# Attention scores of two heads at once on the row halves of the PE array, and no stacked copies of the queries

## The chip, the cores and the metric

The kernel runs on one core of one Trainium2 chip. The metric is the time of the whole program on the device, in microseconds (us). Lower is better. "PE" is TensorE, "DVE" VectorE, "ACT" ScalarE, "POOL" GpSimd, "SP" SyncE, which here only starts DMAs.

## The reference, cut to what matters

A pre-norm block: attention with grouped queries and rotary position, then a small quantized feed-forward layer. The change touches only the scores.

```python
B, S, E = (4, 512, 256);  H, KVH, D = (32, 8, 64)
q = (x @ Wq).reshape(b, s, H, D).transpose(0, 2, 1, 3)      # x is layer-normed
k = (x @ Wk).reshape(b, s, KVH, D).transpose(0, 2, 1, 3)
q = apply_rope(q, pos);  k = apply_rope(k, pos)
scores = einsum('bhqd,bhkd->bhqk', q, k) / sqrt(D)          # each k head serves 4 q heads
scores = where(causal, scores, finfo.min)
out = einsum('bhqk,bhkd->bhqd', softmax(scores), v) ...  @ Wo
```

A head has 64 dimensions, so the sum that makes one score runs over 64 values, while the PE array has 128 rows.

## The kernel before

**Work.** There are 32 steps, one for each batch and each group of four query heads that share one key head. A step has 16 units: four query tiles of 128 queries by four heads. The query tiles are taken in the order 0, 3, 2, 1 (`QUERY_TILES`, L21), and causality lets tile i see (i+1)*128 keys, so units 0 to 3 have n = 128 score columns, 4 to 7 have 512, 8 to 11 have 384 and 12 to 15 have 256. Two steps (`par` 0 and 1) make one pass of a loop, and buffers alternate with `par`.

**Precision.** The scores are wanted at nearly full float32 from products that keep fewer bits (type float32r). So queries and keys are each split in a high and a low part. `kT` holds the keys of the step on 128 partitions, as a high and a low tile. The 64 key dimensions are there twice, in partitions 0 to 63 and again in 64 to 127, because the host puts the key weights twice into the weight matrix. One projection tile j (0 or 1) of the queries holds two heads, 2j in partitions 0 to 63 and 2j+1 in 64 to 127.

**The stack.** Before, `keep_high` (ACT, L637) and `keep_low` (POOL, L351) write the two query parts to a staging area in `wv` (`query_parts`, L95). `place_queries` (SP, L247 to L260) then copies, with four DMAs for a tile, so that `qT[:, h, :]` has the high part of head h in partitions 0 to 63 and the low part in 64 to 127. One product over 128 rows with the high keys (L476) then gives (q_high + q_low) k_high, and a second (L477) gives (q_high + q_low) k_low. A third product (L478, bfloat16, 128 columns) adds the causal mask.

**A unit's way.** PE makes the scores into one of four banks `s_bank`. DVE takes the row maxima (L856). ACT makes the exponentials (L664), and reads the sums. PE transposes the probabilities (`turn`, L490). ACT keeps their high part (L673), DVE the low part (L849). PE multiplies them with the values (`attend`, L503). After every fourth unit DVE normalises the output of the query tile (L865, L870), PE transposes it (`turn_output`, L515), ACT and DVE split it (L681, L878), PE multiplies it with the output weights (`out_product`, at L410), and DVE adds the product to the residual (L888).

**Order.** Each engine's order is written out by hand. In unit u of a step PE issues `scores(u+3)` (LAG is 3; from u = 13 on these are units 0, 1, 2 of the next step), `turn(u)`, at u = 0, 4, 8, 12 the `out_product` of an earlier tile, `attend(u-2)`, at u = 1, 2, 5 the projection of tile 0, 1 or 2 of the next step (`project`, at L410), and at u = 2, 6, 10, 14 `turn_output`. DVE issues at u `keep_probT_low(u-1)` and `maxima(u+3)`. ACT issues `keep_probT(u)`, `exponentials(u+2)`, and after a projection `keep_raw` (L625), which moves it out of the single bank `x_bank`. `project`, `out_product` and `keep_raw` share that bank in turn. A projected tile is rotated: SP swaps its halves (L244), DVE multiplies by the cosines (L818), POOL by the sines (L342) and adds (L345).

**Waits of the scores.** `scores(u)` waits until the exponentials of unit u-4 have read the bank (`exp_done >= U-3`), at u = 0 for the low part of the keys, at u = 0 and 2 for the stacked queries (`q_placed`).

Of the kernel before, what the change touches and what calls it, by code (L numbers as in the profile page):

```python
# [7 lines left out]
GROUP_HEADS = HEADS // KV_HEADS  # L8
LN_EPS, QUANT_EPS, QUANT_MAX = 1e-5, 1e-7, 127.0
P = 128  # L10
# [6 lines left out]
KEYS = 2  # L17
# [33 lines left out]
def attention_ffn_kernel(nc: bass.Bass, x: bass.AP, w_group: bass.AP, w_value: bass.AP, w_out: bass.AP,  # L51
# [9 lines left out]
    with ctx:  # L61
# [6 lines left out]
        def sem(name):  # L68
            return ctx.enter_context(nc.semaphore(name))
# [24 lines left out]
        swp = [sb(f"swp{n}", [P, SEQ], f32)[:, :] for n in range(PROJ_TILES)]  # L94
        def query_parts(it, par, j):  # L95


            if isinstance(it, int) and (it, par) == (0, 0):
                return qT[1][:, j, :], qT[1][:, 2 + j, :]
            return wv[:, HI, j, :], wv[:, LO, j, :]  # L100

# [57 lines left out]
        rope_first, rope_second, rope_done, hi_kept, lo_kept = sem("rope_first"), sem("rope_second"), sem("rope_done"), sem("hi_kept"), sem("lo_kept")  # L159
        q_placed = [sem(f"q_placed{n}") for n in range(2)]  # L160
        scores_done, max_done, exp_done = sem("scores_done"), sem("max_done"), sem("exp_done")
# [27 lines left out]
        def tile_no(it, par, j):  # L189

            return it * (2 * PROJ_TILES) + (PROJ_TILES * par + j), j, it * 2 + par
# [14 lines left out]
        def query_tile(v):  # L206
            return QUERY_TILES[v]
# [11 lines left out]
        def _(sp):  # L219
# [26 lines left out]

            def place_queries(it, par, j):  # L247

                T, _, _ = tile_no(it, par, j)

                sp.wait_ge(lo_kept, T + 1)
                if isinstance(it, int) and (it, par) == (0, 1):
                    sp.wait_ge(q_placed[1 - j], 64)
                    sp.wait_ge(q_placed[j], 64)
                q_hi, q_lo = query_parts(it, par, j)
                for a in range(2):
                    h = 2 * j + a
                    rows = slice(64 * a, 64 * a + 64)
                    sp.dma_start(qT[par][0:64, h, :].bitcast(f32), q_hi[rows, :].bitcast(f32)).then_inc(q_placed[j], 16)
                    sp.dma_start(qT[par][64:128, h, :].bitcast(f32), q_lo[rows, :].bitcast(f32)).then_inc(q_placed[j], 16)  # L260

            def projected(it, par):
                for j in range(PROJ_TILES):
                    swap_halves(it, par, j)
                place_queries(it, par, 0)
                place_queries(it, par, 1)

# [15 lines left out]
        def _(pool):  # L283
# [63 lines left out]
            def keep_low(it, par, j):  # L347
                T, ring, _ = tile_no(it, par, j)
                pool.wait_ge(hi_kept, T + 1)
                high, low = (kT[par][:, HI, :], kT[par][:, LO, :]) if j == KEYS else query_parts(it, par, j)  # L350
                nc.gpsimd.tensor_tensor(low, raw[ring][:, :], high.bitcast(f32), ALU.subtract).then_inc(lo_kept, 1)  # L351
# [44 lines left out]
        def _(pe):  # L396
# [69 lines left out]
            def scores(it, par, u):  # L466
                i, h = query_tile(u // GROUP_HEADS), u % GROUP_HEADS
                U, n = unit_no(it, par, u), (i + 1) * P
                if not (isinstance(U, int) and U < 4):
                    pe.wait_ge(exp_done, U - 3)  # L470
                if u == 0:
                    pe.wait_ge(lo_kept, tile_no(it, par, KEYS)[0] + 1)
                if u in (0, 2):
                    pe.wait_ge(q_placed[h // 2], it * 128 + (64 * par + 64))
                bank, q = s_bank[(par * UNITS + u) % 4], qT[par][:, h, i * P:(i + 1) * P]
                nc.tensor.matmul(bank[:, 0:n], q, kT[par][:, HI, 0:n], start=True, stop=False)  # L476
                nc.tensor.matmul(bank[:, 0:n], q, kT[par][:, LO, 0:n], start=False, stop=False)  # L477
                nc.tensor.matmul(bank[:, i * P:n], ident_b[:, :], mask[:, :], start=False, stop=True)\  # L478
                    .then_inc(scores_done, 1)

# [44 lines left out]
            pe.wait_ge(xT_lo, TOK_TILES)  # L525
            for u in range(LAG):
                scores(0, 0, u)

            def step(it, par, first, last):
# [3 lines left out]
                for u in range(UNITS):  # L533
                    if u + LAG < UNITS:
                        scores(it, par, u + LAG)
                    elif not last:
                        scores(nit, npar, u + LAG - UNITS)
# [61 lines left out]
        def _(act):  # L599
# [28 lines left out]
            def keep_high(it, par, j):  # L628
                T, ring, _ = tile_no(it, par, j)
                act.wait_ge(rope_done, T + 1)  # L630
                if not (isinstance(it, int) and it == 0):
                    act.wait_ge(scores_done, unit_no(it, par, -UNITS))

                if j < KEYS and not (isinstance(T, int) and T < PROJ_TILES):
                    act.wait_ge(q_placed[j], it * 128 + 64 * par)
                dst = kT[par][:, HI, :] if j == KEYS else query_parts(it, par, j)[0]
                nc.scalar.activation(dst, raw[ring][:, :], ACT.Copy).then_inc(hi_kept, 1)  # L637
# [379 lines left out]
```

## Time and profile before

| what | value |
|---|---|
| time, median of 3 runs | 1007.95 us (1007.88 to 1008.24) |
| profiled execution, first to last instruction | 1007.3 us |
| PE busy | 864.6 us (86%), 8488 products and 8488 weight loads |
| DVE busy | 788.5 us (78%) |
| ACT busy | 670.0 us (67%) |
| POOL busy | 564.7 us (56%) |
| stacking copies (`qT<-wv` and `qT<-qT`) | 256 DMAs of 128 KB, 2.3 us each from issue to landing |
| scores on PE, L476, L477, L478 | 195.3, 164.7 and 117.8 us in the records |

The page gives no time for the profiled execution other than its span, which is 0.65 us below the median of the runs. Products on PE are pipelined, so that the duration in a record includes the way through the array and overlaps the next product. What a product costs is the distance between the start of its record and the start of the next one. "PEld" is the load of the weights (the stationary operand), which runs beside products. "Idle before" is the time that an engine stood still ahead of an instruction, with what ended it.

### The profile page before, as it was taken

What the parts mean: (1) busy time and instruction counts of PE and PEld (TensorE: products, weight loads), DVE (VectorE), ACT (ScalarE), POOL (GpSimd) and SP (SyncE); (2) the same over time, 40 slices, a digit from 0 to 9 for tenths busy, and PEclk for the clock granted to TensorE, in tenths of its full rate; (3) what the DMA queues carried; (4) which work ended last, traced back from release to release, by engine and by line L of the source; (5) the groups of instructions that cost most, each with busy time, mean ns of one, the idle gap of its engine ahead of it and who ended that gap; (6) DMA issues with size and microseconds to landing.
All of it is one profiled execution on the core that took longest, in us unless ns stands there. A gap on an engine that the chain in (4) does not pass through costs nothing.

```text
span 1007.3 us, 28110 instructions
## 1 busy us (share of the span) xinstructions
PE 864.6 (86%) x8488; PEld 699.2 (69%) x8488; DVE 788.5 (78%) x1869; ACT 670.0 (67%) x1954; POOL 564.7 (56%) x492
## 2 busy tenths in 40 slices
PE   2978999899999999999999999999999999998732
PEld 1757777677777777777777777777777777777511
DVE  5768878777877787887777777878777777778797
ACT  1557777676667677777766676777767766777533
POOL 4146666555566666655555656666555556554026
PEclk7899999999999999999999999999999999999855
DMA  7134334333333333343433343343434333432002
GB/s 232 42 83 92 91 80 95 74 88 78 86 91 90 82 86 91 78 93 74 91 76 88 89 91 83 81 94 78 94 73 92 75 88 89 91 70 64 2 17 68
DMA packets 52302, 83.58 MB, mean 83 GB/s; under 512 B 12592, under 2 KB 19504, under 8 KB 52272
## 3 DMA queue, kind: packets, MB, share of 16 engines
q1 hardware_dynamic: 46640, 66.43, 28.2%
q0 software_dynamic: 5632, 16.78, 6.8%
q8 instruction: 15, 0.25, 0.1%
q14 instruction: 15, 0.12, 0.0%
HBM read 18.15 MB, written 2.10 MB: 20 GB/s over the span
## 4 chain that ended last, share of the span: by engine, by line
PE 43%; DVE 28%; issue 18%; ACT 6%; DMA 2%; DVEq 1%; POOL 1%; SPq 1%; ACTq 1%; POOLq 0%
PE x_bank L410 20%; DVE probT L849 8%; PE t_bank L490 6%; DVE neg_max L856 6%; PE o_bank L503 4%; PE s_bank L476 4%; PE s_bank L477 3%; DVE raw L818 3%; ACT oT L681 2%; DVE resid L888 2%; DVE o_norm L870 2%; PE t_bank L515 2%; PE t_bank L410 1%; ACT wv L637 1%; PE s_bank L478 1%
## 5 line engine op out<-in xcount | busy, mean ns | idle before, releaser
L673 ACT ACTIVATE probT<-t_bank 128x384 f16<-128x384 f32 (+3 forms) x512 | 224.0, 438 | 159.2 <-PE t_bank L490 157.6
L856 DVE TENSOR_REDUCE neg_max<-s_bank 128x1 f32<-128x384 f32 (+3 forms) x512 | 246.3, 481 | 34.1 <-PE s_bank L478 33.1
L664 ACT ACTIVATE prob<-s_bank,neg_max 128x384 f32<-128x384 f32 (+3 forms) x512 | 267.6, 523 | 0.0
L490 PE MATMUL t_bank<-ident,prob 128*128 128x128 f32 x1280 | 230.7, 278 | 42.7 <-DVE probT L849 36.4
L849 DVE SCALAR_TENSOR_TENSOR probT<-t_bank,probT 128x384 f16<-128x384 f32 (+3 forms) x512 | 246.4, 481 | 7.9 <-ACT probT L673 3.6
L342 POOL TENSOR_TENSOR swp<-swp,sin 128x512 f32<-128x512 f32 x96 | 124.5, 1297 | 166.7 <-DMA swp<-raw 166.5
L503 PE MATMUL o_bank<-vg,probT 128*128 128x64 f16 x3840 | 197.2, 193 | 16.7 <-DVE o_norm L870 15.9
L476 PE MATMUL s_bank<-kT,qT 128*128 128x384 f32 (+3 forms) x512 | 195.3, 381 | 1.2 <-DMA qT<-wv 1.2
L503 PEld LDWEIGHTS o_bank<-vg,probT 128*128 128x128 f16 x3840 | 166.9, 98 | 41.2 <-DVE o_norm L870 26.6
L490 PEld LDWEIGHTS t_bank<-ident,prob 128*128 128x128 f32 x1280 | 138.0, 141 | 58.3 <-ACT prob L664 41.3
L410 PE MATMUL x_bank<-xT,wg 128*128 (+1 forms) x576 | 159.4, 412 | 13.7 <-DVE resid L888 12.1
L345 POOL TENSOR_TENSOR raw<-raw,swp 128x512 f32<-128x512 f32 x96 | 122.2, 1273 | 79.7 <-DVE raw L818 79.5
L477 PE MATMUL s_bank<-kT,qT 128*128 128x384 f32 (+3 forms) x512 | 164.7, 322 | 0.0
L878 DVE TENSOR_TENSOR oT<-t_bank,oT 128x256 fp32r<-128x256 f32 x128 | 54.3, 424 | 103.6 <-ACT oT L681 103.4
L410 PEld LDWEIGHTS x_bank<-xT,wg 128*128 128x128 f32 x576 | 102.0, 189 | 39.5 <-DVE resid L888 15.7
L410 PE MATMUL x_bank<-wo,oT 128*128 (+1 forms) x768 | 123.3, 296 | 5.6 <-DVE oT L878 3.7
L625 ACT ACTIVATE raw<-x_bank 128x512 f32<-128x512 f32 x96 | 57.4, 598 | 92.4 <-PE x_bank L410 92.3
L478 PE MATMUL s_bank<-mask,ident_b 128*128 128x128 bf16 x512 | 117.8, 230 | 0.0
L818 DVE TENSOR_TENSOR raw<-raw,cos 128x512 f32<-128x512 f32 x96 | 114.7, 1195 | 0.8 <-DMA swp<-raw 0.8
L302 POOL DMA_DIRECT2D vg<-value x64 | 48.3, 759 | 110.7 <-PE o_bank L503 105.8
L410 PEld LDWEIGHTS x_bank<-wo,oT 128*128 128x128 f32 x768 | 100.4, 191 | 8.2 <-issue 8.2
L664 ACT ACTIVATION_READ_ACCUMULATOR prob<-s_bank,neg_max 128x1 f32 x512 | 103.7, 203 | 0.0
(87 smaller groups left out, 1082.4 us busy)
## 6 DMA issues: line engine op xcount, KB each, us to landing
qT<-wv SPq DMA_DIRECT2D x248, 128.0 KB, 2.3
swp<-raw SPq DMA_DIRECT2D x384, 64.0 KB, 2.0
wg_raw<-in_w_group POOLq DMA_DIRECT2D x32, 384.0 KB, 3.6
vg<-value POOLq DMA_DIRECT2D x64, 64.0 KB, 2.4
resid<-in_x SPq DMA_DIRECT2D x4, 512.0 KB, 10.5
out<-resid SPq DMA_DIRECT2D x16, 128.0 KB, 1.7
prob<-in_w_out SPq DMA_DIRECT2D x6, 256.0 KB, 7.8
qT<-qT SPq DMA_DIRECT2D x8, 128.0 KB, 2.3
```

The costliest lines, as they stand in the source:

```text
L342: nc.gpsimd.tensor_tensor(swp[ring][:, :], swp[ring][:, :], sin[:, :], ALU.mult).then_inc(rope_second, 1)
L410: last = nc.tensor.matmul(out_ap, left(a, k), right(b, k), start=(k == 0 and (a, b) == (HI, HI)), stop=(k == n - 1 and (a, b) == (LO, HI)))
L476: nc.tensor.matmul(bank[:, 0:n], q, kT[par][:, HI, 0:n], start=True, stop=False)
L477: nc.tensor.matmul(bank[:, 0:n], q, kT[par][:, LO, 0:n], start=False, stop=False)
L478: nc.tensor.matmul(bank[:, i * P:n], ident_b[:, :], mask[:, :], start=False, stop=True)\
L490: last = nc.tensor.transpose(unit_bank(u)[:, k * P:(k + 1) * P], prob[u % 4][:, k * P:(k + 1) * P], ident[:, :])
L503: last = nc.tensor.matmul(o_bank[:, h * HEAD_DIM:(h + 1) * HEAD_DIM], probT[ring][:, a, k * P:(k + 1) * P], vg[par][:, b, k, :], start=(k ...
L664: nc.scalar.activation(prob[u % 4][:, 0:n], s_bank[slot % 4][:, 0:n], ACT.Exp, bias=neg_max[:, slot % 4:slot % 4 + 1], accum_out=row_sum[: ...
L673: nc.scalar.activation(probT[u % 4][:, HI, 0:n], unit_bank(u)[:, 0:n], ACT.Copy, scale=PROB_SCALE).then_inc(probT_hi, 1)
L818: nc.vector.tensor_tensor(raw[ring][:, :], raw[ring][:, :], cos[:, :], ALU.mult).then_inc(rope_first, 1)
L849: nc.vector.scalar_tensor_tensor(out=probT[u % 4][:, LO, 0:n], in0=unit_bank(u)[:, 0:n], scalar=PROB_SCALE, in1=probT[u % 4][:, HI, 0:n], ...
L856: nc.vector.tensor_reduce(neg_max[:, slot:slot + 1], s_bank[slot][:, 0:n], AX.X, ALU.max, negate=True).then_inc(max_done, 1)
```

## The change

`scores` handles two units (two heads of one projection tile) in one call, at odd u only. For each of the two heads it makes three products over 64 rows: high by high, high by low, low by high. The product low by low is no longer made. Head 2j uses partitions 0 to 63 of `qT` and `kT`, head 2j+1 partitions 64 to 127, each with its own bank, and the products of the two alternate. The two mask products follow. `keep_high` and `keep_low` write straight into `qT` (now the high tiles j, then the low tiles 2+j), the staging in `wv`, the DMAs of `place_queries` and the semaphores `q_placed` are gone. The wait for free banks asks for one more finished exponential (`exp_done >= U-2`).

```diff
-        def query_parts(it, par, j):
-            if isinstance(it, int) and (it, par) == (0, 0):
-                return qT[1][:, j, :], qT[1][:, 2 + j, :]
-            return wv[:, HI, j, :], wv[:, LO, j, :]
+        def query_parts(par, j):
+            return qT[par][:, j, :], qT[par][:, 2 + j, :]
...
             def projected(it, par):
                 for j in range(PROJ_TILES):
                     swap_halves(it, par, j)
-                place_queries(it, par, 0)
-                place_queries(it, par, 1)
...
             def scores(it, par, u):
-                i, h = query_tile(u // GROUP_HEADS), u % GROUP_HEADS
+                i, j = query_tile(u // GROUP_HEADS), u % GROUP_HEADS // 2
                 U, n = unit_no(it, par, u), (i + 1) * P
                 if not (isinstance(U, int) and U < 4):
-                    pe.wait_ge(exp_done, U - 3)
-                if u == 0:
-                    pe.wait_ge(lo_kept, tile_no(it, par, KEYS)[0] + 1)
+                    pe.wait_ge(exp_done, U - 2)
                 if u in (0, 2):
-                    pe.wait_ge(q_placed[h // 2], it * 128 + (64 * par + 64))
-                bank, q = s_bank[(par * UNITS + u) % 4], qT[par][:, h, i * P:(i + 1) * P]
-                nc.tensor.matmul(bank[:, 0:n], q, kT[par][:, HI, 0:n], start=True, stop=False)
-                nc.tensor.matmul(bank[:, 0:n], q, kT[par][:, LO, 0:n], start=False, stop=False)
-                nc.tensor.matmul(bank[:, i * P:n], ident_b[:, :], mask[:, :], start=False, stop=True)\
-                    .then_inc(scores_done, 1)
+                    pe.wait_ge(lo_kept, tile_no(it, par, KEYS if u == 0 else j)[0] + 1)
+                banks = [s_bank[(par * UNITS + u + a) % 4] for a in range(2)]
+                cols = slice(i * P, (i + 1) * P)
+                for q_part, k_part in ((HI, HI), (HI, LO), (LO, HI)):
+                    for a in range(2):
+                        rows = slice(64 * a, 64 * a + 64)
+                        nc.tensor.matmul(banks[a][:, 0:n], qT[par][rows, 2 * q_part + j, cols], kT[par][rows, k_part, 0:n],
+                                         start=(q_part, k_part) == (HI, HI), stop=False)
+                for a in range(2):
+                    nc.tensor.matmul(banks[a][:, i * P:n], ident_b[:, :], mask[:, :], start=False, stop=True)\
+                        .then_inc(scores_done, 1)
...
-            for u in range(LAG):
+            for u in (0, 2):
                 scores(0, 0, u)
...
-                    if u + LAG < UNITS:
+                    if u % 2 == 1 and u + LAG < UNITS:
                         scores(it, par, u + LAG)
-                    elif not last:
+                    elif u % 2 == 1 and not last:
                         scores(nit, npar, u + LAG - UNITS)
...
-                if j < KEYS and not (isinstance(T, int) and T < PROJ_TILES):
-                    act.wait_ge(q_placed[j], it * 128 + 64 * par)
```

## Rows read from the trace of the kernel before

**Rows 1.** The page: busy time, share of the span and instructions of each engine.

```profile
PE 864.6 (86%) x8488; PEld 699.2 (69%) x8488; DVE 788.5 (78%) x1869; ACT 670.0 (67%) x1954; POOL 564.7 (56%) x492
```

**Rows 2.** By stretch: length; busy PE, PEld, DVE, ACT, POOL; clock; DMA share; GB/s.

```profile
92.80:922.50 829.70, 760.14 (x7737) 623.62 (x7735) 654.41 (x1530) 585.35 (x1740) 503.12 (x418) 1.00 0.37 85
...
509.40:518.80 9.40, 9.15 (x74) 7.14 (x75) 4.90 (x15) 5.38 (x20) 2.90 (x4) 1.00 0.30 76
518.80:533.40 14.60, 12.64 (x134) 10.28 (x134) 13.71 (x27) 11.29 (x31) 10.11 (x9) 1.00 0.34 77
533.40:537.10 3.70, 3.67 (x51) 3.42 (x51) 2.95 (x9) 2.62 (x10) 3.62 (x3) 1.00 0.64 142
```

**Rows 3.** Timeline of PE, scores with 512, 128, 384, 256 columns: start, us, what.

```profile
517.79 0.47 PE L476 MATMUL s_bank<-kT,qT 128*128 128x512 f32 x1
518.10 0.40 PE L477 MATMUL s_bank<-kT,qT 128*128 128x512 f32 x1
518.34 0.23 PE L478 MATMUL s_bank<-mask,ident_b 128*128 128x128 bf16 x1
518.41 0.28 PE L490 MATMUL t_bank<-ident,prob 128*128 128x128 f32 x1
...
508.55 0.31 PE L476 MATMUL s_bank<-kT,qT 128*128 128x128 f32 x1
...
508.88 0.39 PE L490 MATMUL t_bank<-ident,prob 128*128 128x128 f32 x2
...
520.68 0.42 PE L476 MATMUL s_bank<-kT,qT 128*128 128x384 f32 x1
...
521.18 0.60 PE L490 MATMUL t_bank<-ident,prob 128*128 128x128 f32 x4
...
528.98 0.36 PE L476 MATMUL s_bank<-kT,qT 128*128 128x256 f32 x1
...
529.37 0.50 PE L490 MATMUL t_bank<-ident,prob 128*128 128x128 f32 x3
```

**Rows 4.** Timeline of weight loads: two score loads, and products on alternating column halves.

```profile
517.76 0.19 PEld L476 LDWEIGHTS s_bank<-kT,qT 128*128 128x128 f32 x1
517.87 0.19 PEld L477 LDWEIGHTS s_bank<-kT,qT 128*128 128x128 f32 x1
...
19.09 1.87 PE L443 MATMUL x_bank<-ident,swp 128*64 128x1 f32 x32 [9.87 <-DVE swp L783]
```

**Rows 5.** Timelines and waits about `x_bank`, 515.5 to 518.9.

```profile
515.50 0.60 ACT L625 ACTIVATE raw<-x_bank 128x512 f32<-128x512 f32 x1 [1.24 <-PE x_bank L410]
...
516.15 1.23 PEld L410 LDWEIGHTS x_bank<-xT,wg 128*128 128x128 f32 x6 [0.16 <-ACT raw L625]
...
PEld x_bank L410 <- ACT raw L625: 4.2, 26, 0.2
...
518.83 0.42 DVE L878 TENSOR_TENSOR oT<-t_bank,oT 128x256 fp32r<-128x256 f32 x1 [2.00 <-ACT oT L681]
```

**Rows 6.** Timelines of PE at unit 11, and of DVE at unit 13.

```profile
532.74 0.36 PE L476 MATMUL s_bank<-kT,qT 128*128 128x256 f32 x1
...
533.43 0.52 PE L490 MATMUL t_bank<-ident,prob 128*128 128x128 f32 x3
...
508.75 0.18 DVE L865 RECIPROCAL row_inv<-row_sum 128x4 f32<-128x4 f32 x1
```

**Rows 7.** Timelines of ACT and DVE about unit 6.

```profile
524.81 0.60 ACT L673 ACTIVATE probT<-t_bank 128x512 f16<-128x512 f32 x1 [0.18 <-PE t_bank L490]
...
526.79 0.42 DVE L878 TENSOR_TENSOR oT<-t_bank,oT 128x256 fp32r<-128x256 f32 x1 [0.66 <-ACT oT L681]
```

**Rows 8.** Timelines of ACT and PE, unit 15's exponential and scores(2) of the next step.

```profile
509.13 0.20 ACT L664 ACTIVATION_READ_ACCUMULATOR prob<-s_bank,neg_max 128x1 f32 x1
...
509.97 0.30 PE L476 MATMUL s_bank<-kT,qT 128*128 128x128 f32 x1
```

**Rows 9.** Waits for the stacked queries over the whole span: us, times, longest.

```profile
PE s_bank L476 <- DMA qT<-wv: 1.2, 2, 0.7
```

More of the change, by code:

```diff
@@ L159, in attention_ffn_kernel @@
         rope_first, rope_second, rope_done, hi_kept, lo_kept = sem("rope_first"), sem("rope_second"), sem("rope_done"), sem("hi_kept"), sem("lo_kept")
-        q_placed = [sem(f"q_placed{n}") for n in range(2)]
         scores_done, max_done, exp_done = sem("scores_done"), sem("max_done"), sem("exp_done")
@@ L245, in swap_halves @@
                         .then_inc(swapped[ring], 16)
[L247 to L260, printed above, removed]
             def projected(it, par):
@@ L349, in keep_low @@
                 pool.wait_ge(hi_kept, T + 1)
-                high, low = (kT[par][:, HI, :], kT[par][:, LO, :]) if j == KEYS else query_parts(it, par, j)
+                high, low = (kT[par][:, HI, :], kT[par][:, LO, :]) if j == KEYS else query_parts(par, j)
                 nc.gpsimd.tensor_tensor(low, raw[ring][:, :], high.bitcast(f32), ALU.subtract).then_inc(lo_kept, 1)
@@ L632, in keep_high @@
                     act.wait_ge(scores_done, unit_no(it, par, -UNITS))
-                if j < KEYS and not (isinstance(T, int) and T < PROJ_TILES):
-                    act.wait_ge(q_placed[j], it * 128 + 64 * par)
-                dst = kT[par][:, HI, :] if j == KEYS else query_parts(it, par, j)[0]
+                dst = kT[par][:, HI, :] if j == KEYS else query_parts(par, j)[0]
                 nc.scalar.activation(dst, raw[ring][:, :], ACT.Copy).then_inc(hi_kept, 1)
```

## The prediction

> **What bounds the kernel now.** I first read the busy shares of the whole span: PE leads with 86%, DVE has 78% [rows 1]. Such a mean can hide who waits for whom, so next come the busy times by stretch. From 92.8 to 922.5 us the kernel runs 30 equal steps, 829.7/30 = 27.66 us each, with PE busy for 92% of the time at a granted clock of 1.00, that is 2.4 GHz [rows 2]. One step falls in three stretches. From 509.4 to 518.8 PE is busy for 9.15 of 9.40 us and DVE for 4.90: PE sets the pace, with the output product and two projections in it. From 518.8 to 533.4 DVE is busy for 13.71 of 14.60 us: DVE sets the pace and PE has slack. In the last 3.7 us both are near full. So a saving on PE counts in the first stretch and partly in the last, and 14.6 of 27.7 us hardly react to it.
>
> **What the scores cost now.** I read start to start, since a product's record overlaps the next. With n = 512 the sequence is 517.79, 518.10, 518.34, 518.41: the first product takes 0.31 us (0.08 of it the exposed load of its weights), the second 0.24, the mask 0.07, together 0.62. With 128, 384 and 256 columns the whole unit takes 0.33, 0.50 and 0.39 [rows 3]. Two heads therefore cost 0.66 (n = 128), 0.78 (256), 1.00 (384) and 1.24 us (512). The columns alone take about 0.23 us at 512 (0.24 less a 0.01 to 0.02 seam), so 0.45 ns each: 0.06, 0.12, 0.17, 0.23.
>
> **The change on PE.** A pair now has six products over 64 rows and two masks, where it had four products and two masks. Two prices are not in the trace, because it has no product over 64 rows.
>
> First, whether the two heads' products run at the same time. Lower end: fully, the pair streams 3n columns. Upper end: not at all, 6n columns.
>
> Second, the load of weights for 64 rows. Two loads of 128 columns start 0.11 us apart (517.76, 517.87). Nearest to the new load is the row of 32 products that alternate between the two column halves and load 64 columns each: (1.87 - 0.25)/31 = 0.052 us from one to the next. Loads there go by their columns, and one after the other, although the halves are different [rows 4]. The new loads keep 128 columns, so one after the other they cost 6 x 0.11 = 0.66 us for a pair. Lower end: the two halves load side by side, 3 x 0.11.
>
> I take heads side by side, loads one after the other. Then a pair costs 0.66, plus the last product's columns (0.06 to 0.23), plus two masks 0.14: **0.86, 0.92, 0.97 and 1.03 us** for 128, 256, 384, 512. Against now: +0.20, +0.14, -0.03, -0.21. For all eight pairs of a step that is 2 x 0.10 = +0.2 us, nearly nothing. The page "TensorE: Matmul & The Clock Gate" of the Trainium skill (Part 3) has matmuls on different row groups starting about 4 ns apart; no run here shows that yet. By it alone, with loads hidden, a pair would cost what the first rival below has. That page (LDWEIGHTS) also gives the load time by columns and not by rows.
>
> **Where the pairs lie.** The order matters more than the sum. Scores come at odd u only, and for two units.
> - *First stretch.* The pair (2,3) replaces units 2 and 3, both on PE's path (0.86 - 0.76, as 2 and 3 took 0.42 and 0.34 start to start in this stretch): +0.10. The pair (4,5) comes at u = 1, ahead of the first projection, in place of unit 4 alone: 1.03 - 0.62 = +0.41. Unit 5 no longer stands between the first and second projection, but that frees nothing. ACT begins to empty `x_bank` at 515.50, once the first projection is out, takes 0.60 us, and only then, at 516.15, does the next projection load. It waited for ACT in 26 steps already, though by only 0.16 us [rows 5]. Unit 5 filled that hole, and now PE stands idle in it. What follows the projections is ACT's move of the output and then DVE at 518.83, which waited 2.00 us for it [rows 5]. So the stretch gets longer by 0.51. In some steps PE has small gaps of 0.2 to 0.3 us ahead of the output product and the first projection, which take up part; I count **+0.35**.
> - *Second stretch.* Pairs (6,7), (8,9), (10,11), (12,13) lie where PE waits for DVE; costed at nothing, the cover being DVE's 13.7 us. If they took 1.6 us each, the maxima of unit 6 and the projection at u = 5 would be late. One gain: at u = 6 no scores stand ahead of the transposes. ACT waited 0.18 us for those at 524.81, and DVE later 0.66 us for the split [rows 7]: **-0.20**.
> - *Last stretch.* The pair (14,15) costs 0.92 ahead of `turn(11)`. Unit 14 alone took 0.38, and to the transposes at 533.43 there were 0.31 us of slack [rows 6]: +0.22. Unit 15 (0.39) is no longer ahead of the output product: -0.39. The pair (0,1) is then ahead of `attend(11)`, where unit 0 alone was: 0.86 - 0.33 = +0.53. DVE needs `attend(11)` for its reciprocal at 508.75 [rows 6], with no slack that I can count on. Sum +0.36; I count **+0.30**, since DVE has a tenth or so to spare.
>
> Sum +0.45 us a step, over 31 steps (the last has no successor) +14 us.
>
> **Waits and queues.** The new wait for the exponentials of unit u, ahead of scores(u+3), has behind it on PE `turn(u)`, which waits for the same event, so only the pair itself can come late. In the step that I followed it is closest at u = 15: ACT ends at 509.33, PE comes to the scores at 509.97 [rows 8]. Costed at nothing; if ACT fell behind, PE would have no scores to fill with, a few tenths at 8 places a step. Eight DMAs a step leave SP's queue behind the swaps, and ACT's wait for them. Scores waited for such a copy twice in the whole run, 1.2 us together [rows 9]: -1 us. The halves swapped by DMA may land earlier with less traffic, but DVE takes them late in its own order: nothing.
>
> The sum: +14 - 1 = +13. Against the profiled span of 1007.3 us, which lies 0.65 us below the median of the runs, this gives 1020.3, and beside the median **1021 us**.
>
> **Rivals.**
> 1. *Loads side by side (the faster side).* Decides from a load price of 0.055 us a load and below. A pair is then 0.08 + 3 x max(0.11, columns) + 0.14 = 0.55, 0.58, 0.73, 0.91. First stretch: -0.21 + 0.29 = +0.08. Last: (14,15) fits into the slack, -0.39, and +0.22 = -0.17. Middle -0.20. Sum -0.29 x 31 = -9, with the copies -10: 998 us. For it: the halves read different partitions. Against it: the 0.052 us of [rows 4].
> 2. *The array has to run empty at each change between 128 and 64 rows.* A mask's record lasts 0.23 us while the next product starts 0.07 later [rows 3], so the way out of the array is at most 0.16 us beyond. Two changes for each of three pairs on the path: 6 x 0.16 = 0.96 us a step, +30 us: 1051, or 1028 on top of rival 1. Against it: a mask in bfloat16 follows a float32 product with a seam of only about 0.02 us, but both use all rows. The page "TensorEngine Tiling (Array Packing)" of the Trainium skill (Key Properties) states this rule: a change of tiling mode drains TensorE. No row here shows such a change in the steady steps.
> 3. *It doesn't do what it says: the two heads' products run one after the other.* A pair is 0.66 + 0.06 + 0.14 = 0.86 (128), 0.94, 1.24 and 6 x 0.23 + 0.22 = 1.60 (512). The pair (4,5) then costs +0.98 and (2,3) +0.10; (6,7) and the pair ahead of the third projection come some 0.3 late each; the last stretch +0.4. With -0.2 this is about +1.75 x 31 = +54: 1061 us. Against it: the rows don't overlap, nor do the banks.
>
> A drop of the clock is no case: it stands at 1.00 with PE at 92% [rows 2], and PE's work hardly changes.
>
> **Chances.** Forecast 0.34, rival 1 0.27, rival 2 (with either load price) 0.20, rival 3 0.12, and 0.07 for what I misjudge in the path, both ways. Measurements tell 0.2%, about 2 us, from no change. Faster: most of rival 1, and the part of the forecast in which shifts that I priced at +0.45 are gained back by PE's greater slack at even u: 0.36. Within 0.2%: 0.09. Slower: 0.55. The range takes in both load prices, the small end of rival 2 and most of its large one: 988 to 1052. The likeliest case alone would be 1008 to 1032.
>
> **What the profile after would show.** Right: products with `64*` rows for two heads starting close together, loads 0.11 us apart, pairs of 0.86 to 1.03 us start to start, PE idle ahead of the second projection by some 0.5 us with ACT's `keep_raw` as the releaser, and steps of about 28.1 us. Wrong towards faster: loads of the two halves starting together, pairs of 512 columns under 0.95 us. Wrong towards slower: a gap of more than 0.1 us ahead of the first 64-row load or ahead of the mask (rival 2), or a distance of two product lengths between two loads of one head (rival 3). The forecast also falls if PE waits for ACT's exponentials ahead of the pairs, or if DVE's busy share in the second stretch falls under 90%.

## The result, and the profile after

The changed kernel takes **1033.6 us** (median of 4 runs, 1031.6 to 1037.4) against 1008.1 before: ratio 1.0256, interval 1.0237 to 1.0275. The direction was forecast; the size was not: +25.5 us where the sum said +13. The profiled execution is the run of 1031.6 us, with a span of 1029.9 against 1007.3, so 22.6 us are to be found in the traces.

The page of the changed kernel, busy shares and the granted clock in 40 slices:

```profile
PE 870.5 (85%) x9000; PEld 683.9 (66%) x9000; DVE 793.2 (77%) x1869; ACT 653.3 (63%) x1954; POOL 563.7 (55%) x492
...
PEclk7989999999999999999999999999999999999955
```

Against [rows 1], PE has 512 more products but is busy for only 6 us more; nothing else moved much. The slices are too coarse for the clock. The windows of the changed kernel, with the columns of [rows 2], show it: 4 us ahead of a fall and the fall itself, twice.

```profile
227.81:231.81 4.00, 2.64 (x37) 1.88 (x35) 3.79 (x9) 2.75 (x9) 2.90 (x4) 1.00 0.00 0
231.80:235.20 3.40, 3.40 (x30) 3.23 (x29) 1.65 (x4) 1.93 (x7) 3.32 (x3) 0.51 0.00 0
...
285.84:289.84 4.00, 2.63 (x37) 1.86 (x36) 3.71 (x9) 2.75 (x9) 2.90 (x4) 1.00 0.00 0
289.90:293.20 3.30, 3.30 (x30) 3.14 (x29) 1.73 (x5) 1.79 (x6) 3.22 (x3) 0.50 0.00 0
```

From 231.8 on the clock is at 0.5, which is 1.2 GHz, and it had been at 2.4 GHz. Ahead of that PE was busy for 2.64 of 4.00 us. There are five such falls in the 30 steady steps; the kernel before has none there. All five have the same place in the step: they begin 2.2 to 2.4 us behind the start of `turn(10)`. The timeline of PE there, in the changed kernel (the same place in a later step, without a fall) and in the kernel before:

```profile
542.80 0.51 PE L486 MATMUL o_bank<-vg,probT 128*128 128x64 f16 x12
544.34 0.52 PE L473 MATMUL t_bank<-ident,prob 128*128 128x128 f32 x3 [1.02 <-DVE probT L829]
545.12 0.44 PE L486 MATMUL o_bank<-vg,probT 128*128 128x64 f16 x9 [0.27 <-DVE o_norm L850]
```

```profile
531.29 0.52 PE L490 MATMUL t_bank<-ident,prob 128*128 128x128 f32 x3 [0.69 <-DVE probT L849]
```

The hole ahead of `turn(10)` is 1.05 us long in the mean of the changed kernel's 30 steps, and 0.63 in those of the kernel before.

I took the length of a step as the distance between two of POOL's `kT` rows (L351 before, L330 after). Without a fall it is 28.16 us, against 27.68: **+0.48 a step, 31 x 0.48 = 15 us**. The steps with a fall last about 29.85, 1.7 more: **5 x 1.7 = 8 us**. Together 23 of 22.6. The other three runs of the changed kernel show mean clocks of 0.949 to 0.954 where this one has 0.956, and the slower the clock the longer the run (0.949 goes with 1037.4). The number of falls spreads the times: this trace and those of e3, e6 and e8 below have 5, 11, 2 and 7 falls in runs of 1031.6, 1041.2, 1027.3 and 1035.6 us, and less 1.7 us a fall all four come to 1022.5 to 1023.9.

**The pairs.** Timeline of PE in the changed kernel, pairs of 512 and 128 columns, and of its weight loads:

```profile
525.27 0.35 PE L486 MATMUL o_bank<-vg,probT 128*128 128x64 f16 x6
525.55 0.96 PE L458 MATMUL s_bank<-kT,qT 64*128 64x512 f32 x6
526.44 0.29 PE L461 MATMUL s_bank<-mask,ident_b 128*128 128x128 bf16 x2
526.57 0.28 PE L473 MATMUL t_bank<-ident,prob 128*128 128x128 f32 x1
...
550.91 0.44 PE L498 MATMUL t_bank<-ident,o_norm 128*128 128x128 f32 x2
551.28 0.55 PE L458 MATMUL s_bank<-kT,qT 64*128 64x128 f32 x6
551.76 0.28 PE L461 MATMUL s_bank<-mask,ident_b 128*128 128x128 bf16 x2
551.88 0.39 PE L473 MATMUL t_bank<-ident,prob 128*128 128x128 f32 x2
```

```profile
531.05 0.19 PEld L458 LDWEIGHTS s_bank<-kT,qT 64*128 64x128 f32 x2 [0.17 <-issue]
531.05 0.53 PEld L458 LDWEIGHTS s_bank<-kT,qT 64*128 64x128 f32 x6 [0.17 <-issue]
551.28 0.41 PEld L458 LDWEIGHTS s_bank<-kT,qT 64*128 64x128 f32 x6 [0.17 <-issue]
```

Two loads lie within the time of one (x2 in 0.19 us), and six take 0.41 us where one after the other they would need 5 x 0.11 + 0.19 = 0.74. So **both halves load side by side, and their products run side by side**: a pair costs 0.60, 0.68, 0.85 and 1.02 us from start to start (128, 256, 384, 512 columns), where six products of 512 columns in a row would take 1.38. But ahead of each pair PE loses time that no wait explains. The last product before a pair and the pair's first two, in the changed kernel behind `attend` and behind `turn_output`, then the same behind `attend` in the kernel before:

```profile
525.42 0.19 PE L486 MATMUL o_bank<-vg,probT 128*128 128x64 f16 x1
525.55 0.50 PE L458 MATMUL s_bank<-kT,qT 64*128 64x512 f32 x2
...
551.08 0.27 PE L498 MATMUL t_bank<-ident,o_norm 128*128 128x128 f32 x1
551.28 0.33 PE L458 MATMUL s_bank<-kT,qT 64*128 64x128 f32 x2
```

```profile
518.58 0.19 PE L503 MATMUL o_bank<-vg,probT 128*128 128x64 f16 x1
518.61 0.48 PE L476 MATMUL s_bank<-kT,qT 128*128 128x512 f32 x1
```

From start to start that is 0.12 us behind `attend` and 0.20 behind `turn_output` (medians of the records), against 0.03 in the kernel before: 0.09 and 0.17 us more. Four of the eight pairs follow `attend`, the four (2,3), (6,7), (10,11) and (14,15) follow `turn_output`. With this way in, a pair costs 0.70 or 0.78 us at 128 columns, 0.77 or 0.85 at 256, 0.94 or 1.02 at 384 and 1.11 or 1.19 at 512, against 0.66, 0.78, 1.00 and 1.24 for two 128-row units [rows 3]. The eight pairs of a step sum to 7.4 us either way.

**Where the steps grew.** Starts of some instructions after POOL's `kT` row, mean of the undisturbed steps between 300 and 470 us (five in each trace), worked out from the timelines:

| instruction | before | changed | shift |
|---|---|---|---|
| turn_output, PE (u = 14) | 4.32 | 4.47 | +0.15 |
| first projection, PE | 7.99 | 8.56 | +0.57 |
| second projection, PE | 10.39 | 10.96 | +0.57 |
| split of the output, DVE (u = 3) | 13.07 | 13.64 | +0.57 |
| third residual add, DVE | 16.04 | 16.57 | +0.53 |
| fourth split of the output, DVE | 21.04 | 21.24 | +0.20 |
| third rotation, DVE | 22.91 | 23.36 | +0.45 |
| fourth residual add, DVE | 24.49 | 25.02 | +0.53 |

The shift arises between `turn_output` and the first projection, where the pairs (2,3) and (4,5) stand, and stays. The hole ahead of the second projection is there. Timeline of PE and the sum of its waits, changed kernel:

```profile
529.25 1.66 PE L389 MATMUL x_bank<-xT,wg 128*128 x6 [0.57 <-ACT raw L608]
...
PE x_bank L389 <- ACT raw L608: 17.2, 31, 0.6
```

### The profile page after: what moved, and what is told of

It is laid out like the page before. It is cut to its first block, busy times and chain, and to the rows that moved or that the text cites. A ratio compares the mean times of both kernels' runs of the same rounds, so it can differ in the third digit from the quotient of the medians.

```text
span 1029.9 us, 28776 instructions
## 1 busy us (share of the span) xinstructions
PE 870.5 (85%) x9000; PEld 683.9 (66%) x9000; DVE 793.2 (77%) x1869; ACT 653.3 (63%) x1954; POOL 563.7 (55%) x492
## 4 chain that ended last, share of the span: by engine, by line
PE 48%; DVE 29%; issue 15%; ACT 5%; DMA 1%; DVEq 1%; POOL 0%; SPq 0%; ACTq 0%; POOLq 0%
PE x_bank L389 15%; PE s_bank L458 10%; DVE neg_max L836 8%; DVE probT L829 7%; PE o_bank L486 7%; PE t_bank L473 7%; PE s_bank L461 3%; DVE raw L798 3%; PE t_bank L498 3%; DVE o_norm L850 3%; ACT raw L608 2%; ACT probT L653 2%; PE t_bank L389 2%; DVE row_inv L845 1%; DMA resid<-in_x 1%
## 5 line engine op out<-in xcount | busy, mean ns | idle before, releaser
L473 PE MATMUL t_bank<-ident,prob 128*128 128x128 f32 x1280 | 235.1, 282 | 46.8 <-DVE probT L829 43.7
L644 ACT ACTIVATE prob<-s_bank,neg_max 128x384 f32<-128x384 f32 (+3 forms) x512 | 270.5, 528 | 0.0
L486 PE MATMUL o_bank<-vg,probT 128*128 128x64 f16 x3840 | 199.8, 195 | 27.2 <-DVE o_norm L850 26.4
L458 PE MATMUL s_bank<-kT,qT 64*128 64x128 f32 (+3 forms) x1536 | 188.3, 350 | 0.4 <-ACT prob L644 0.4
L473 PEld LDWEIGHTS t_bank<-ident,prob 128*128 128x128 f32 x1280 | 141.8, 143 | 63.5 <-ACT prob L644 43.5
L458 PEld LDWEIGHTS s_bank<-kT,qT 64*128 64x128 f32 x1536 | 114.5, 185 | 31.9 <-issue 15.6
L389 PE MATMUL x_bank<-wo,oT 128*128 (+1 forms) x768 | 126.7, 301 | 5.8 <-DVE oT L858 3.7
L389 PEld LDWEIGHTS x_bank<-wo,oT 128*128 128x128 f32 x768 | 103.1, 195 | 10.4 <-issue 8.2
L644 ACT ACTIVATION_READ_ACCUMULATOR prob<-s_bank,neg_max 128x1 f32 x512 | 106.5, 208 | 0.0
L330 POOL TENSOR_TENSOR qT<-raw,qT 128x512 fp32r<-128x512 f32 x64 | 81.6, 1276 | 0.0
```

The source lines that it names most:

```text
L389: last = nc.tensor.matmul(out_ap, left(a, k), right(b, k), start=(k == 0 and (a, b) == (HI, HI)), stop=(k == n - 1 and (a, b) == (LO, HI)))
L458: nc.tensor.matmul(banks[a][:, 0:n], qT[par][rows, 2 * q_part + j, cols], kT[par][rows, k_part, 0:n], start=(q_part, k_part) == (HI, HI), ...
L473: last = nc.tensor.transpose(unit_bank(u)[:, k * P:(k + 1) * P], prob[u % 4][:, k * P:(k + 1) * P], ident[:, :])
L486: last = nc.tensor.matmul(o_bank[:, h * HEAD_DIM:(h + 1) * HEAD_DIM], probT[ring][:, a, k * P:(k + 1) * P], vg[par][:, b, k, :], start=(k ...
L644: nc.scalar.activation(prob[u % 4][:, 0:n], s_bank[slot % 4][:, 0:n], ACT.Exp, bias=neg_max[:, slot % 4:slot % 4 + 1], accum_out=row_sum[: ...
```

## The experiments

All were timed against the kernel before on the same chip. Steps are means without falls, in the trace of each.

**e1: the order alone.** In the kernel before:

```diff
-                    pe.wait_ge(exp_done, U - 3)
+                    pe.wait_ge(exp_done, U - 2)
...
+                for a in range(2):   # the same three products, for heads h and h + 1
...
-                    if u + LAG < UNITS:
+                    if u % 2 == 1 and u + LAG < UNITS:
```

> The kernel before (stacked queries, 128-row products, the copies) with one thing of the change: scores of two units at once, at odd u, with the later wait for the exponential. Theory A (order and rows both cost): by the path of the prediction the pairs (now 0.66, 0.78, 1.00, 1.24 us) add about +0.35 us a step, +11 us, 1019; PE stands idle 0.4 to 0.6 us ahead of the second projection with ACT's keep_raw as releaser. Rival B (the order is free, everything comes from the change between 128 and 64 rows): 1008 to 1010. On the clock: if the falls to half speed in the changed kernel come from the order, they show here too (mean clock under 0.958); if they come from products on half of the rows, the clock stays at 0.960.

1029.4 us, ratio 1.0216 (1.0191 to 1.0241), steps 28.25. Nearly the whole loss is there without a single 64-row product. The step grows by 0.57, more than the 0.35 that I gave it, and B falls. The clock has no fall in the 30 steady steps, though PE has the same hole in each, 1.05 us in the mean. It falls once in the last step, at 944.9 us, behind waits of 0.57 us for DVE and 0.90 for a stacking copy. The timeline of PE in e1, its hole and the projection:

```profile
526.76 1.71 PE L410 MATMUL x_bank<-xT,wg 128*128 x6 [0.56 <-ACT raw L626]
...
541.91 0.52 PE L491 MATMUL t_bank<-ident,prob 128*128 128x128 f32 x3 [1.05 <-DVE probT L850]
```

**e2: the same without copies.** In the changed kernel the six products become, for each head, two over all rows (`qT[par][:, 2 * k_part + j, cols]` by `kT[par][:, k_part, 0:n]`). The scores are then of two heads summed and lack the mixed terms.

> The changed kernel with its order, its layout and no copies, but the products over all 128 rows (two for a head, high by high and low by low, so the scores are of two heads summed and lack the mixed terms: part of the computation is changed). Against the run before it only the copies and the waits for them are gone. Theory A: the copies cost nothing, the same time within 2 us. Rival: the copies slow the other transfers or ACT, then 3 us or more faster. Against the changed kernel it says what 64 rows cost by themselves: by the pair prices of the trace after with 0.17 us of gap ahead (0.77, 0.85, 1.02, 1.19) about 5 to 8 us, and the falls of the clock if half rows make them.

1026.2 us, ratio 1.0176 (1.0155 to 1.0197), steps 28.20. One fall, in the last but one step, has nearly the place of the changed kernel's, 1.4 us behind the start of `turn(10)`, whose hole is the longest of this trace. Windows and timeline of e2:

```profile
931.90:935.90 4.00, 2.46 (x36) 1.99 (x35) 3.96 (x9) 2.78 (x9) 3.31 (x3) 1.00 0.00 0
936.10:939.40 3.30, 3.30 (x24) 3.05 (x23) 1.82 (x5) 1.89 (x6) 1.41 (x2) 0.50 0.03 7
...
934.55 0.52 PE L471 MATMUL t_bank<-ident,prob 128*128 128x128 f32 x3 [1.18 <-DVE probT L827]
```

Against e1 the copies are worth about 3 us, within what the two intervals leave open; half of it is steps of 0.05 us less. The changed kernel has steps of 28.16, so **in an undisturbed step 64-row pairs gain and lose nothing against 128-row pairs**. They add falls: 5 here against 1 in e2 and none in e1.

**e3: head after head.** The loops over `a` and over the parts are exchanged.

> The changed kernel with the six products of a pair in the order head A three times, head B three times. Theory A (the halves really work at the same time, but PE starts products in order): only the third of A and the first of B overlap, so a pair of 512 columns goes from 1.02 to about 1.5 us and one of 128 from 0.60 to about 0.8; +0.8 us or more a step on the path, 1055 to 1075. Rival (the products of two heads never overlap, the order of the six means nothing): 1029 to 1037, like the changed kernel.

1037.4 us, ratio 1.0279 (1.0252 to 1.0305), 11 falls in the trace. The pairs keep their price, 1.02 us at 512 columns and 0.61 at 128, and the steps are 28.15. Theory A is wrong: the pair doesn't behave as if its products started one after the other as written. The records don't say which head a product belongs to, so it isn't shown whether PE took head B's ahead or the order had changed on the way to it. The rival's reason is wrong too: the loads of the two halves start together here as well, 0.01 us apart (timeline of e3's loads and of its PE):

```profile
555.64 0.19 PEld L458 LDWEIGHTS s_bank<-kT,qT 64*128 64x128 f32 x2
...
555.64 0.97 PE L458 MATMUL s_bank<-kT,qT 64*128 64x512 f32 x6
556.54 0.29 PE L461 MATMUL s_bank<-mask,ident_b 128*128 128x128 bf16 x2
```

**e4: one more change of rows in each pair.** The two masks come after the first two products.

> The changed kernel with the two mask products (128 rows) after the first two 64-row products instead of at the end: one more change from 64 to 128 rows and back in each pair, the same products. Theory A (PE runs empty at such a change, 0.1 to 0.17 us each): each pair is 0.25 to 0.35 us longer, three or four pairs a step lie on the path, +25 to +40 us, 1055 to 1075. Rival (the gaps of 0.17 us ahead of the pairs are something else, a change of rows is free): within 3 us of the changed kernel.

1048.4 us, ratio 1.0405 (1.0388 to 1.0423), steps 28.79, no falls. Timeline of PE in e4, a pair of 128 columns:

```profile
555.29 0.33 PE L461 MATMUL s_bank<-kT,qT 64*128 64x128 f32 x2
555.55 0.29 PE L458 MATMUL s_bank<-mask,ident_b 128*128 128x128 bf16 x2
555.76 0.44 PE L461 MATMUL s_bank<-kT,qT 64*128 64x128 f32 x4
556.13 0.44 PE L475 MATMUL t_bank<-ident,prob 128*128 128x128 f32 x2
```

555.29 to 556.13 is 0.84 us, against 0.60 in the changed kernel; at 512 columns 1.31 against 1.02. So one more way to 128 rows and back costs 0.24 to 0.29 us. The total grew by 15 and not 25 us. The falls are gone, as is the hole at `turn(10)` (0.04 us in the mean), and DVE's rotations take 0.83 us in the mean instead of 1.20 (see e5), so that the price of a change is read from the pairs and not from the total.

**e5: the pair (4,5) behind the first projection.** In the changed kernel:

```diff
+                    if u == 2:
+                        scores(it, par, 4)      # PE; no longer at u == 1
...
+                    if u == 1 and not first:    # DVE, ahead of maxima(u + LAG)
+                        normalise_output(*query_part(it, par, u // 4 - 1))
```

> The changed kernel with the pair (4,5) issued at u = 2, behind the first projection, in the time in which ACT empties x_bank, and DVE normalising the output ahead of the maxima of unit 4. Theory A (the markers of the traces: nearly all of the +0.53 us a step arises between turn_output and the first projection, where this pair stands): the first projection starts 1.1 us earlier in a step, the second about 0.6 earlier, steps go from 28.1 to 27.5 to 27.7 us, 1010 to 1018 with some falls of the clock, about 1008 without. Rival (something else in the order of pairs, the DVE stretch or the last one, takes the time back): steps of 28 us or more, 1026 or more.

**989.9 us, ratio 0.9824 (0.9807 to 0.9840)**: faster than both kernels by far, steps 27.06, no fall, all runs within 0.8 us. My reason was only part of it. From `turn_output` the first projection starts 0.40 us earlier than in the changed kernel (3.69 us after it, not 4.09), but the second no earlier at all (6.48 against 6.49). The step lost 1.10 us, so something else gave. The traces point at DVE's rotations; e9 and e10 test that. Timelines of DVE and POOL at the third rotation, first the changed kernel, then e5:

```profile
427.38 1.28 POOL L321 TENSOR_TENSOR swp<-swp,sin 128x512 f32<-128x512 f32 x1 [0.40 <-DMA swp<-raw]
427.44 1.77 DVE L798 TENSOR_TENSOR raw<-raw,cos 128x512 f32<-128x512 f32 x1
```

```profile
438.26 0.69 DVE L801 TENSOR_TENSOR raw<-raw,cos 128x512 f32<-128x512 f32 x1
438.31 1.78 POOL L321 TENSOR_TENSOR swp<-swp,sin 128x512 f32<-128x512 f32 x1 [0.61 <-DMA swp<-raw]
```

Whoever starts first keeps its time, and the other is held up for most of it: DVE started 0.06 us after POOL and took 1.77 us instead of 0.69; POOL started 0.05 us after DVE and took 1.78 instead of 1.28. In the kernel before, all 62 rotations of the first and third place in a step, 1.30 and 1.61 us in the mean, overlap POOL's product by the sines, and the 29 that overlap nothing of POOL take 0.68. The groups of the page's kind, DVE's rotation in the kernel before, the changed kernel and e5:

```profile
L818 DVE TENSOR_TENSOR raw<-raw,cos 128x512 f32<-128x512 f32 x96 | 114.7, 1195 | 0.8 <-DMA swp<-raw 0.8
```

```profile
L798 DVE TENSOR_TENSOR raw<-raw,cos 128x512 f32<-128x512 f32 x96 | 115.5, 1203 | 0.8 <-DMA swp<-raw 0.8
```

```profile
L801 DVE TENSOR_TENSOR raw<-raw,cos 128x512 f32<-128x512 f32 x96 | 75.1, 783 | 0.5
```

40 us less of DVE's time, 1.3 a step, in the stretch that DVE leads. The page "GPSIMD Engine Reference" of the Trainium skill (Specifications, the table at its start) says that POOL shares its SBUF interfaces with VectorE, in contention with instructions that have two SBUF inputs; the rotation has two, and this case's traces agree. The hole ahead of `turn(10)`, which is DVE's lateness, closes with it: PE's wait there is 2.1 us in 800 us of e5 against 38.8 in the changed kernel, and the clock stays up.

**e6: DVE's part of e5 alone.**

> Control for the run before: the changed kernel with only DVE's part of that edit, the output normalised ahead of the maxima of unit 4 at u = 1. Theory A (the pair's place decides): the same as the changed kernel within 2 us, steps of 28.1. Rival (the late normalisation, +0.56 us in the markers, is what holds the step up): steps of 27.8 or less, 8 us or more faster.

1033.2 us, ratio 1.0281 (1.0229 to 1.0332), steps 28.18, two falls in the trace, which is of the fastest run. No effect; the runs spread from 1027 to 1042.

**e7: a filler.** `scores` at u = 4 begins with one product over 128 rows and 512 columns.

> The changed kernel with one more product over all 128 rows with 512 columns ahead of the pair (4,5), into its bank, which the pair then overwrites. Theory A (the clock falls because the stretch ahead of the first projection gives PE too little work, part of it on half of the rows): no fall in the 30 steady steps, mean clock 0.960 or more; the product costs 0.25 to 0.3 us a step on the path, so steps of 28.4 and 1030 to 1033, the same time as the changed kernel, with less spread between runs (2 us instead of 6). Rival (the falls have another cause): as many falls, and 1038 to 1045.

1044.7 us, ratio 1.0376 (1.0351 to 1.0401), steps 28.53, four falls. The price is as expected, but the falls stay. The filler stands ahead of the first projection, and the windows of the changed kernel show the fall behind `turn(10)`, 11 us earlier in the order: it was put in the wrong place and says nothing on the cause.

**e8: the changed kernel again**, on the chip of e5 to e7.

> The changed kernel itself on the chip of these runs, to see how the number of falls of the clock varies: steps of 28.1 to 28.2 us wherever the clock holds, 2 to 10 falls of 3.4 us, 1.6 to 1.7 us each, and a total of 1023 plus these, 1028 to 1038.

1032.3 us, ratio 1.0237 (1.0218 to 1.0256), steps 28.14, seven falls in the trace (a run of 1035.6).

**e9: PE's part of e5 alone.**

> The changed kernel with only PE's part of the edit that gave 990 us: the pair (4,5) behind the first projection, DVE's order as it was. Theory A (the place of the pair frees PE's path, and DVE's order decides whether it can be used): the output is normalised about 1 us later, attend(0) and the second projection with it, steps of 28 us or more. Theory C (the 990 us come mostly from rotations on DVE, 0.68 us instead of 1.3 and 1.7, because they no longer start while POOL multiplies): the time follows the mean of DVE's rotation, 0.8 us with steps near 27, 1.2 us with steps near 28.

1031.7 us, ratio 1.0235 (1.0198 to 1.0272), steps 28.44. Rotations of 0.68 to 0.73 us in all three places, and steps longer than the changed kernel's: fast rotations alone are not the cause, and theory C falls in this form. The output is normalised 3.5 us later than in e5, and the second projection starts 1.36 us later, behind `attend(0)`, as A had it. e5 needs both halves of its edit. There is no hole at `turn(10)` and no fall in the steady steps; the one fall of the trace is in the first step, which still has the hole (1.19 us).

**e10, e11, e12: POOL multiplies only after DVE.** The same edit in the changed kernel, in the kernel before and in e5:

```diff
                 pool.wait_ge(swapped[ring], use * 64 + 64)
+                pool.wait_ge(rope_first, T + 1)
                 nc.gpsimd.tensor_tensor(swp[ring][:, :], swp[ring][:, :], sin[:, :], ALU.mult).then_inc(rope_second, 1)
                 pool.wait_ge(rope_second, T + 1)
-                pool.wait_ge(rope_first, T + 1)
```

> The changed kernel with POOL's wait for DVE's rotation put ahead of its own multiplication, so that the two never run on a tile at once. Pair and order of PE untouched. Theory C (DVE stands still while POOL multiplies, 0.6 us in the first and 1.0 us in the third rotation of a step, on the path of DVE's stretch): DVE's rotations take 0.68 us, steps go from 28.15 to 26.8 to 27.3 us, 1033 to about 995 to 1005. Rival (DVE has slack there, or POOL becomes late and holds up keys and queries): within 5 us of the changed kernel.

> The kernel before with the same edit on POOL. Theory C: rotations of 0.68 us, steps from 27.6 to 26.3 to 26.8 us, 970 to 985, so that it stays ahead of the changed kernel with the same edit by 15 to 25 us, and the order of the pairs is what the change costs. Rival: the kernel before keeps its time, because its steps are bound elsewhere.

> The 990 us kernel (pair (4,5) behind the projection, normalising first) with the same edit on POOL. Theory C: its rotations are already 0.9, 0.68 and 0.69 us, so it gains at most 0.2 us a step: 984 to 990. If the place of the pairs costs nothing any more, it is as fast as the kernel before with that edit; if the pairs at odd u still cost, it stays behind by 5 us or more. Rival: POOL's later start delays the keys, 992 or more.

| | time, ratio (interval) | step | mean rotation | falls |
|---|---|---|---|---|
| e10, changed | 1008.3, 1.0009 (0.9995 to 1.0023) | 27.62 | 0.79 | 0 |
| e11, before | 995.2, 0.9861 (0.9834 to 0.9888) | 27.13 | 0.92 | 1 |
| e12, e5 | 1005.7, 0.9979 (0.9965 to 0.9993) | 27.54 | 0.79 | 0 |

The edit is worth about 0.55 us a step to both kernels, less than C said. It doesn't remove the collision whole: the first two rotations take 0.68 us, but the third 1.06 (e10) and 1.39 (e11), and it overlaps POOL's `keep_low` there. With it eased, 0.49 us a step and 13 us remain between the two: this is what the change costs apart from the falls, and by e1 and e2 it is the order of the pairs. The 0.54 us that e10 gains are half of e5's 1.10; no run isolates the other half. The changed kernel gains 24 us from the edit, 17 by its steps and the rest by the falls, which go when the hole shrinks (0.23 us in e10). The fall of e11 has another place, behind `turn_output` of unit 14, where PE waited for a stacking copy. Windows and timeline of e11:

```profile
175.20:179.20 4.00, 2.45 (x26) 1.75 (x25) 2.34 (x8) 2.22 (x10) 2.32 (x2) 1.00 0.49 111
179.20:182.60 3.40, 3.40 (x23) 2.72 (x24) 1.30 (x4) 0.67 (x5) 0.00 (x0) 0.51 0.16 66
...
177.61 0.30 PE L476 MATMUL s_bank<-kT,qT 128*128 128x128 f32 x1 [1.25 <-DMA qT<-wv]
```

In e12 the edit costs 16 us. POOL waits for DVE there for 222.6 us in 800 us, against 192.9 in e10, and the fourth residual add comes 0.3 us late against e5; which link makes the other delay wasn't followed.

**e13: both edits of e5 in the kernel before**, with single units. **e14: e5 with stacked queries, copies and 128-row products.**

> The kernel before, single units and 128-row products, with the two edits of the 990 us kernel: the scores of unit 4 behind the first projection (then ahead of those of unit 5) and the output normalised ahead of the maxima of unit 4. Theory D (the 64-row pairs have no part in the 990 us, only the place of the scores and DVE's order): 985 to 998. Rival E (the pairs matter, since they leave the even units free): 1003 or more, no better than the kernel before.

> The 990 us order (pairs at odd u, (4,5) behind the first projection, normalising first) with stacked queries, copies and 128-row products. Theory D: the pairs cost start to start the same with 64 as with 128 rows once the gap ahead is counted (0.77 against 0.62 at 128 columns, 1.19 against 1.21 at 512), and the copies some 0.1 us a step, so 988 to 996, like the 990 us kernel. Rival E (64-row pairs save time where PE leads, at 384 and 512 columns): 5 us or more slower than the 990 us kernel.

e13: 1005.1 us, ratio 0.9968 (0.9954 to 0.9982), steps 27.64, rotations still 1.07 us. e14: **989.4 us, ratio 0.9818 (0.9800 to 0.9835)**, steps 27.07, rotations 0.77. So D holds where it speaks of rows: e14 is as fast as e5 with none of the 64-row products. It fails in e13: single units don't get there. What gave 990 us is two units at a time at odd u, with one pair moved behind the projection, and rotations that happen to lose less time to POOL. How much each of the three is worth by itself isn't shown.

## Why the prediction was right and wrong

- *What bounds the kernel*: right. The stretches keep their leaders, and the shift arises in the one that PE leads. But I read DVE's stretch as work of fixed length. Its rotations were 1.30, 0.68 and 1.61 us long before, and the excess, about 1.5 us a step, is a stall against POOL that I looked past. The changed kernel has it too, so it is no part of the 25 us.
- *The load price*: wrong. "Loads there go by their columns, and one after the other, although the halves are different", from two halves of columns. The row halves load side by side. And [rows 4] was misread: in that row the loads to the two column halves start together as well, and the granted clock is 0.50. Two loads come together every (1.87 - 0.25)/15 = 0.11 us, at 1.2 GHz, and the mean of 0.052 hid the pairs; read so, the row spoke for rival 1. By itself rival 1 had the right products: 0.55, 0.58, 0.73, 0.91 against 0.60, 0.68, 0.85, 1.02, which hold about 0.1 us of way out ahead of the masks. Timeline of the first loads of that row, cut at 19.10 and at 19.25, and the window around them, kernel before:

```profile
19.09 0.19 PEld L443 LDWEIGHTS x_bank<-ident,swp 128*64 128x64 f32 x2 [11.03 <-DVE swp L783]
19.09 0.29 PEld L443 LDWEIGHTS x_bank<-ident,swp 128*64 128x64 f32 x4 [11.03 <-DVE swp L783]
...
19.00:21.00 2.00, 1.87 (x32) 1.79 (x32) 1.76 (x4) 0.74 (x2) 0.00 (x0) 0.50 0.72 244
```

- *The change of rows*: rival 2, at 0.20, was right in kind and nearly in price: at most 0.16 us was said for each change, 0.09 or 0.17 is lost ahead of a pair, and e4 has 0.24 to 0.29 for a further two changes. The rule of "TensorEngine Tiling (Array Packing)" of the Trainium skill (Key Properties), that a change of tiling mode drains TensorE, agrees. Rival 1 with rival 2 gave 1028. In the forecast the two errors, loads priced too high and changes left out, hid each other by luck: the pairs (2,3) and (4,5) were put at 0.86 + 1.03 = 1.89 us and cost 0.78 + 1.11 = 1.89.
- *The place of the pairs*: right in kind. First stretch +0.35 was said, +0.42 measured between `turn_output` and the first projection, with 0.57 us of hole ahead of the second. The last stretch was said at +0.30 and gave +0.15: `turn(11)` comes 0.17 us later behind POOL's `kT` row (0.22 was said), `turn(12)` 0.24 earlier, and what was too large is the pair (0,1), put at 0.86 where it costs 0.70. The middle was said at -0.20, and 0.3 us did appear at the fourth split, but the third rotation and the residual add behind it took it back. The sum, +0.45 against +0.48, is better than its terms, which is luck.
- *Copies*: -1 us was said; 3 between e1 and e2.
- *The clock*: this is the step that failed. "A drop of the clock is no case: it stands at 1.00 with PE at 92%". The mean of 30 steps hid where PE's holes are. With scores at odd u only, no scores fill the hole at `turn(10)`: PE waited there 0.63 us in the mean before and 1.05 after. In the kernel before, the scores of unit 13 stood in it. The term put at nothing is five falls, 8 us, in this trace, and more in the longer runs. The steps gave +15 us where the sum had +14, so that without the falls the run would be at about 1023, beside the 1021 forecast.

What of the falls is shown: the falls of the changed kernel come behind that hole, and where it is closed or short (e4, e5, e9, e10, e12, e14) the steady steps have none. The kernels with the hole and 64-row products (the changed one twice, e3, e6, e7) fall 29 times in 150 steady steps, e1 and e2, with the same hole but products over 128 rows, once in 60. So 64-row products make the falls far more frequent, but they aren't needed for one: e2 and e11 fall without them, where PE had waited 1.18 and 1.25 us, and e1 does in its last step. In the 4 us ahead of a fall PE was busy for 2.46 us in e2 and 2.45 in e11, and for 2.6 to 2.7 in 28 of the 29 others. Which property of the 64-row products counts, their halved rows or something else in the way they keep PE busy, and why only some of the steps with the hole fall, no run tells.

## What to carry to other kernels

Count what a product costs together with its way in and out: two heads on the row halves took 18% off the products of a 512-column pair but only 4 to 10% off the pair with its way in, and added time at 128 columns. Before grouping work on an engine that others follow, ask which hole each piece filled: here the grouping cost 15 us, and moving one pair and one of DVE's instructions by one place turned the whole loss into a gain of 18. And read the spread of one instruction's durations: 0.68 and 1.7 us for the same shape is a stall; easing it gave the kernel before 12 us, where the whole change cost it 25.

## What the runs showed of the hardware that I had not expected

- Loads of 128 float32 columns to the two row halves start together (x2 in 0.19 us). So do loads of 64 columns to the two column halves (x2 in 0.19, x4 in 0.29 us, at a granted clock of 0.50).
- Products of the two halves overlap even if they are written head after head: e3's pair of 512 columns takes 1.02 us, as in the changed kernel.
- A change from 128 to 64 rows holds the first product back by 0.09 us behind `attend` and by 0.17 behind `turn_output`.
- DVE's product of two SBUF tiles is held up while POOL's runs, and the reverse: 1.77 for 0.69 us, and 1.78 for 1.28 us, decided by 0.06 us of start.
- The clock fell to 1.2 GHz for 3.4 us behind a hole of 1.0 to 1.25 us in PE's work: often with 64-row products (29 of 150 steps), rarely with 128-row ones (1 of 60 in e1 and e2).
